# A decoder layer on one core: turning feed-forward tiles between output halves, and five smaller moves

## What is computed

```python
x = x + attention(layernorm(x), w_q_down, w_q_up_nope, w_q_up_rope, w_kv_down, w_k_rope, w_uk, w_uv, w_out)
x = x + cross_attention(layernorm(x), ctx_4096)
x = x + feed_forward(layernorm(x), k0, s0, k1, s1, k2, s2)

def feed_forward(x):                 # conn_dense(k, x) = x @ (+1 where k, -1 elsewhere)
    h = relu(s0 * conn_dense(k0, x)) * 2
    h = relu(ei_dense(h, k1, s1)) * 2     # the last fifth of the inputs is scaled by -4
    return ei_dense(h, k2, s2)
```

## Time and profile before

| what | value |
|---|---|
| median of three runs | 2095.1 us (2094.97 to 2096.36) |
| profiled execution: its time, its span | 2096.1 us, 2093.9 us |
| PE busy, PE weight loads busy | 2060.2 us, 1741.1 us |
| DVE, ACT, POOL busy | 1271.5, 775.7, 450.0 us |
| chain that ended last, by engine | PE 95%, DVE 2%, DMA 1%, ACT 1% |
| moved by DMA | 284.8 MB |

### The profile page before, as it was taken

The page is one execution under the profiler, slowest core; times in us unless marked ns, Lnnn a source line. Parts: engine busy times, 40 slices in busy tenths (PEclk is TensorE's granted clock), DMA queues, the critical chain, the costliest instruction groups (busy, mean ns, idle before and its releaser), DMA issues.

```text
span 2093.9 us, 30080 instructions
## 1 busy us (share of the span) xinstructions
PE 2060.2 (98%) x10746; PEld 1741.1 (83%) x10746; DVE 1271.5 (61%) x2114; ACT 775.7 (37%) x2018; POOL 450.0 (21%) x406
## 2 busy tenths in 40 slices
PE   6999999999999999999999999999999999999999
PEld 5787888888888888888888888888888868888887
DVE  4636666666666666666666666666667772333321
ACT  3324444444434353433333333333333455232221
POOL 2013333333324142321111211112121211000000
PEclk9999999999999999999999999999999999999999
DMA  5516343535353452666524234342444381202010
GB/s 211 239 66 224 105 174 105 195 115 205 123 183 121 157 178 100 224 223 215 170 90 150 85 120 135 118 142 70 150 132 184 124 310 49 81 1 81 1 41 40
DMA packets 63018, 284.78 MB, mean 136 GB/s; under 512 B 6641, under 2 KB 7281, under 8 KB 51441
## 3 DMA queue, kind: packets, MB, share of 16 engines
q1 hardware_dynamic: 62960, 284.00, 39.4%
HBM read 172.83 MB, written 111.15 MB: 136 GB/s over the span
## 4 chain that ended last, share of the span: by engine, by line
PE 95%; DVE 2%; DMA 1%; ACT 1%; issue 0%; POOL 0%; DVEq 0%; SPq 0%; POOLq 0%; ACTq 0%
PE at_out L53 11%; PE at_out L54 11%; PE at_out L55 11%; PE at_qbank L53 7%; PE at_qbank L55 7%; PE at_qbank L54 7%; PE at_qbank L967 6%; PE at_qbank L968 6%; PE at_score L756 4%; PE at_score L754 3%; PE at_turned L763 3%; PE at_value L55 2%; PE at_value L54 2%; PE at_value L53 2%; PE at_score L755 1%; PE at_turned L981 1%
## 5 line engine op out<-in xcount | busy, mean ns | idle before, releaser
L1564 DVE TENSOR_TENSOR at_acc<-at_out,at_acc 128x512 f32<-128x512 f32 x512 | 352.1, 688 | 116.0 <-PE at_out L55 109.3
L53 PE MATMUL at_out<-at_wvo,at_val_hi 128*128 128x512 f32 x1024 | 402.7, 393 | 1.7 <-DVE at_acc L1564 1.7
L54 PE MATMUL at_out<-at_wvo,at_val_hi 128*128 128x512 f32 x1024 | 400.9, 391 | 0.0
L55 PE MATMUL at_out<-at_wvo,at_val_lo 128*128 128x512 f32 x1024 | 399.8, 390 | 0.0
L1087 ACT ACTIVATE at_probs<-at_probs,at_row_stats 128x128 f32<-128x128 f32 x512 | 199.8, 391 | 358.4 <-DVE at_row_stats L1542 358.4
L1323 POOL TENSOR_TENSOR at_probs<-at_probs,at_row_stats 128x512 f32<-128x512 f32 x128 | 133.1, 1040 | 592.0 <-DVE at_row_stats L1547 592.0
L55 PEld LDWEIGHTS at_out<-at_wvo,at_val_lo 128*128 128x128 f32 x1024 | 192.3, 188 | 42.9
L53 PEld LDWEIGHTS at_out<-at_wvo,at_val_hi 128*128 128x128 f32 x1024 | 193.0, 188 | 37.0 <-DVE at_acc L1564 3.3
L54 PEld LDWEIGHTS at_out<-at_wvo,at_val_hi 128*128 128x128 f32 x1024 | 192.8, 188 | 32.4
L1093 ACT ACTIVATE at_pT_hi<-at_turned 128x512 fp32r<-128x512 f32 x128 | 76.4, 597 | 318.6 <-PE at_turned L763 318.6
L756 PE MATMUL at_score<-at_tok,at_qrope 128*128 128x256 f32 x512 | 170.5, 333 | 0.0
(11 more groups left out here) (193 smaller groups left out, 4344.1 us busy)
## 6 DMA issues: line engine op xcount, KB each, us to landing
wvo_d<-at_wvo SPq DMA_DIRECT2D x16, 2048.0 KB, 7.3
parts_d<-at_rope_parts SPq DMA_DIRECT2D x32, 1024.0 KB, 7.0
at_qrope<-parts_d SPq DMA_DIRECT2D x128, 256.0 KB, 5.0
at_wvo<-wvo_d SPq DMA_DIRECT2D x16, 2048.0 KB, 8.4
ab_raw<-in_w_heads SPq DMA_DIRECT2D x32, 576.0 KB, 4.7
cr_ctx<-in_context SPq DMA_DIRECT2D x16, 1024.0 KB, 7.7
wabs_d<-at_wabs SPq DMA_DIRECT2D x16, 768.0 KB, 7.6
at_wabs<-wabs_d SPq DMA_DIRECT2D x16, 768.0 KB, 5.3
```

The lines of the kernel that those rows point to most:

```text
L53: pe.matmul(out, w_hi, x_hi, start=first, stop=False)
L54: pe.matmul(out, w_hi, x_lo, start=False, stop=False)
L55: return pe.matmul(out, w_lo, x_hi, start=False, stop=last)
L1564: dve.tensor_tensor(at, outb[n][:], at, ALU.add).then_inc(added, 1)
```

## The change

Six edits, none of which alters the arithmetic.

1. Feed forward: the transposes of the next chunk's tile `t`, which stood after both output halves of tile `t`, now stand between half 0 and half 1. ACT's copies follow by their waits. DVE's two subtractions and the next tile's normalisation move ahead of the sum of half 1.
2. ACT, slot 0 of the full quads: `take_head` now comes ahead of the split of the rope weights.
3. The last chunk's tiles are stored in two halves of 512 columns, each as soon as it is summed.
4. SP loads all four x tiles ahead of the projection's first piece.
5. ACT takes the root of tile `t + 1` right behind the normalisation of tile `t`, and the first piece of the projection is split after the normalisation of tile 1 and the root of tile 2.
6. DVE: the moments of a first tile are cut into two halves, and the shift of the tile before stands between them.

```diff
             def preparation():                      # SP
-                load_x_tile(0, 0)
-                load_x_tile(0, 1)
+                for t in range(BPC):
+                    load_x_tile(0, t)
                 load_w_down(0)
-                load_x_tile(0, 2)
-                load_x_tile(0, 3)
                 sp.dma_start(ident[:], consts["ident"]).then_inc(ident_in, 16)
...
             for t in range(BPC):                    # SP, last chunk
-                sp.wait_ge(ff_summed, 2 * (BPC * c + t + 1))
-                sp.dma_start(out_chunks[c][:, t, :], ff_x[c % 2][:, t, :]).then_inc(y_out[c], 16)
+                for n in range(2):
+                    cols = slice(n * CH, (n + 1) * CH)
+                    sp.wait_ge(ff_summed, 2 * (BPC * c + t) + n + 1)
+                    sp.dma_start(out_chunks[c][:, t, cols], ff_x[c % 2][:, t, cols]).then_inc(y_out[c], 16)
...
             def feed_output(c, t):                  # PE
                 for n in range(2):
+                    if n and c + 1 < CHUNKS:
+                        for half in range(2):
+                            feed_turn(c + 1, t, half)
                     if t:
                         pe.wait_ge(ff_summed, 2 * BPC * c + 2 * (t - 1) + n + 1)
...
                     for t in range(BPC):
                         feed_output(c, t)
-                        if c + 1 < CHUNKS:
-                            for half in range(2):
-                                feed_turn(c + 1, t, half)
...
             def preparation():                      # ACT
+                root(0, 0)
                 for t in range(BPC):
-                    root(0, t)
                     first_normalise(t)
-                    if t == 0:
+                    if t + 1 < BPC:
+                        root(0, t + 1)
+                    if t == 1:
                         cut_w_down(0)
                 cut_w_down(1)
...
                         take_head(h, use[s] + 1, count)    # ACT, slot
+                if s == 0 and kind == "full":       # these stood ahead of take_pair and take_head
+                    act.wait_ge(wqr_raw_in, 16 * (m + 2))
+                    act.wait_ge(wqr_out, 16 * (m + 2))
+                    act.activation(wqr[:, 0], wqr_raw, ACT.Copy).then_inc(wqr_hi, 1)
...
             def preparation():                      # DVE
                 moments(0, 0)
-                first_shift(0)
-                moments(0, 1)
-                moments(0, 2)
-                first_shift(1)
-                moments(0, 3)
-                first_shift(2)
-                first_shift(3)
+                for t in range(1, BPC):
+                    half_moments(0, t, 0)
+                    first_shift(t - 1)
+                    half_moments(0, t, 1)
+                    whole_moments(0, t)
+                first_shift(BPC - 1)
...
                             dve.scalar_tensor_tensor(...).then_inc(ff_summed, 1)    # DVE, feed
-                        if c + 1 < CHUNKS:
-                            for half in range(2):
-                                feed_turn(c + 1, t, half)
-                            if t + 1 < BPC:
-                                feed_normalise(c + 1, t + 1)
+                            if n == 0 and c + 1 < CHUNKS:
+                                for half in range(2):
+                                    feed_turn(c + 1, t, half)
+                                if t + 1 < BPC:
+                                    feed_normalise(c + 1, t + 1)
```

More of the change, by code:

```diff
@@ L641, in _ @@
             for t in range(BPC):
-                sp.wait_ge(ff_summed, 2 * (BPC * c + t + 1))
-                sp.dma_start(out_chunks[c][:, t, :], ff_x[c % 2][:, t, :]).then_inc(y_out[c], 16)
+                for n in range(2):
+                    cols = slice(n * CH, (n + 1) * CH)
+                    sp.wait_ge(ff_summed, 2 * (BPC * c + t) + n + 1)
+                    sp.dma_start(out_chunks[c][:, t, cols], ff_x[c % 2][:, t, cols]).then_inc(y_out[c], 16)
             sp.wait_ge(y_out[CHUNKS - 2], 16)
-            sp.wait_ge(y_out[CHUNKS - 1], 16 * BPC)
+            sp.wait_ge(y_out[CHUNKS - 1], 16 * 2 * BPC)
         @block.tensor
@@ L1178, in slot @@
                     rope(m + 1, c, 16 * (m + 1 + c))
[L1179 to L1182, removed]
                 if part:
@@ L1435, in _, with half_moments, whole_moments, moments @@
         def _(dve):
[L1436 to L1439, removed]
+            def half_moments(i, t, h):
+                if h == 0:
+                    dve.wait_ge(x_in[i % 2][t], 16 * (i // 2 + 1))
+                dve.bn_stats(stats[:, t % 2, h, :], xt[i % 2][:, t, h * 512:(h + 1) * 512])
+            def whole_moments(i, t):
                 dve.drain()
                 dve.bn_aggr(mv[:, t, :], stats[:, t % 2].rearrange("p h s -> p (h s)")).then_inc(var_ready, 1)
+            def moments(i, t):
+                for h in range(2):
+                    half_moments(i, t, h)
+                whole_moments(i, t)
             def inverse(i, t):
```

## The result

The changed kernel takes 2087.92 us (median of 7 runs, 2086.4 to 2089.93) against 2094.97 us (2094.75 to 2096.36, also 7) on the same chip: ratio 0.9966, 95% interval 0.9955 to 0.9978, or 7.05 us less. The profiled execution took 2087.33 us with a span of 2085.1; against the one of before (2096.1 and 2093.9) that is 8.8 us less.

The account below looks back on a forecast made before the run. TensorE, busy 2060.2 of 2093.9 us, was taken as the bound, leaving 34 us idle to win. Terms 5.4 + 0.6 + 1.0 + 1.15 = 8.2 us took the median from 2095.1 to 2086.9, range 2085.0 to 2089.9.

Parts of the forecast that it names:

- The boundaries: Feed forward, three chunk boundaries: turning between output halves hides a 1.81 us TensorE stall at each, 5.4 us in all.
- the margin of tile 0: Feed forward: tile 0's normalised input is ready 0.6 us before its earlier transposes need it, the edit's smallest margin.
- The tail: End of kernel: storing the last tile in halves leaves 256 KB less to land after the last sum, saving 0.63 us.
- The start: First tiles: the fourth normalisation starts 1.36 us sooner; worth 0.7 to 1.36 us depending on TensorE's clock, taken as 1.0.
- Heads ahead of the split: Slot 1 of quad 0: evicting heads first moves the stall to values and output product, and wins 1.15 us.
- TensorE's release moves from 201.91 to 200.76: 1.15 us: Slot 1 of quad 0: the sums TensorE waits for come 1.15 us sooner, so TensorE goes on that much sooner.
- my second rival: Quad 0: the earlier head-weight store delays the raw rope weights; term -1.3 instead of 1.15, total 2089.4 us; chance 0.10.
- a stall of about 3 us was to remain: Slot 1 of quad 0, sign of being right: about 3 us of stall stays, ahead of values and sums.
- The later full quads: Six other full quads: the split delays ACT's high part by 0.84 us, covered by 2.0 us, so no loss.
- The stall goes whole: Rival, slot 1 of quad 0: the whole stall vanishes if raw weights land some 3 us earlier; 2084.0 us; chance 0.04.
- stall of twelve turns: Rival, feed forward: the normalised tile comes late for all 12 turns, 21.7 us lost, 2114.0 us; chance 0.02.
- wait of L929: Feed forward, sign of being wrong: a wait for the normalised tile; no size given.

Follow-up runs that it names:

- the experiment on the order: Kernel before with the new start order on ACT and VectorE, but x tiles 2 and 3 still loaded behind the projection's first piece: 2094.58 us, ratio 0.9997.
- The heads alone: Kernel before with only the head evictions moved ahead of the rope weights' split on ACT: 2094.41 us, ratio 0.9991.
- turns on TensorE only: Kernel before with TensorE's transposes between the output halves, VectorE keeping its old order with both sums first: 2099.96 us, ratio 1.0023.
- The two kernels with the weights early: Changed kernel with quad 1's raw rope weights issued earlier on SP: 2083.86 us; the same with the split ahead of the heads again: 2083.81 us.

## Why the prediction was right, point by point

The forecast was 2086.9 us, within 2085.0 to 2089.9, and the median is 2087.92.

- **The boundaries (5.4 us).** Right in place and size: 1.89 each in the profiled pair against 1.81, and 1.84 to 1.91 over all profiles. The stall went under half 1 with nothing late next, and the margin of tile 0 was 0.6 us as worked out. The experiment with VectorE's old order shows what the edit rests on: it is VectorE's turn behind the sum of half 0 that makes it work, and TensorE's new order without it loses.
- **The tail (0.63 us).** Right: 0.63 in the profiled pair, and the landing 2.0 us. The Trainium skill, DMA: Bandwidth & Descriptors, section Anatomy of one DMA, gives its numbers for the GpSimd path. With its fixed 2.0 us inside the 2.6 measured, a half would have taken 2.3 us, and the trace shows 2.0, so that fixed part doesn't hold for this queue. The prediction left out the same rule's second part, a time per byte, by which 256 KB less save 0.60 us as an estimate. The trace's 0.63 agrees with that. The size itself is read from traces alone, since the timed comparison is too coarse for it.
- **The start (1.36 us at the transposes, taken as 1.0).** The transposes came 1.56 us sooner, a little more than worked out: the first normalisation started at 7.15 instead of 7.25, and the step with the split took 1.96 instead of 2.05. There was no wait for data, and the experiment on the order shows that this was owed to the loads: without them 1.08 of the 1.56 us are lost to tile 2. What it is worth hung on the clock in the prediction, and the profiles bear that out for the old start only. In the first pair of profiles the rise came 8.64 and 8.57 us behind the transposes, in the second 5.97 and 6.06, so it moved with the start in both; but a third profile of before shows 8.11, so such a delay changes by itself by more than the start moved. In the first pair slot 1 of quad 0 began 1.76 us sooner, which is the whole 1.56 and 0.2 more. Over all profiles, seven with the old start began it at 187.92 to 188.99 (mean 188.44) and six with the new one at 187.04 to 187.39 (mean 187.24), 1.2 us sooner. From the first transposes to that slot the old start took 172.4 and 172.5 us where the rise came 6.5 and 6.0 us behind the transposes, and 172.8 to 173.2 where it came 8.0 to 8.6 behind. With the new start there is no such order: 173.05 with the rise at 8.57 and 173.07 to 173.6 with it at 5.6 to 6.8. The step on the clock is the one that failed here: with the new start an early rise only brings TensorE to a wait for a low part (1.14 us at 24.11 in the second profile of after). The 1.0 taken, the middle of two values for the clock, is near the 1.2 by luck.
- **Heads ahead of the split (1.15 us).** The mechanism was right, the size wrong. ACT stood at the same wait (4.23 us in place of 7.67), the high part started 0.75 us behind the split's start as worked out, and the stall moved to values and output. The sums came sooner by about the predicted amount: counted from the start of the slot, the first output product that waits for them was released at 200.00 - 188.99 = 11.01 us before, and at 197.00 - 187.23 = 9.77 after (9.86 in the second profile), 1.24 and 1.15 sooner.

  The step that failed is the next one, "TensorE's release moves from 201.91 to 200.76: 1.15 us". Between the two releases lie six matmuls, and before they took some 1.5 of the 1.91 us between the releases. After they ran at the low level and took 199.73 - 197.00 = 2.73. So TensorE came to the second place at 12.50 us into the slot, when the sums were there at about 11.7 (VectorE's sum of 198.17 ends at 198.86), and 0.8 of the 1.24 us were given back. In the second profile the fall came later: TensorE was at the second place at 12.11, but stayed at the low level behind it, and from there to the end of the slot it took 6.28 us instead of 5.58.

  Slot 1 took 18.17 and 18.39 us against 18.50, 0.33 and 0.11 less. In the old order the same fall costs nothing that shows, since TensorE waits for sums behind it: in the nine profiles with the old order slot 1 took 18.51 to 18.61 us in the four with a low clock there, and 18.50 to 18.67 in the five without. The heads alone, with the clock at 1.00, gave 17.73, still 0.4 more than the 17.35 worked out. There ACT had the raw weights 7.26 us behind their issue in place of 6.87 before (6.84 to 6.99 in the nine profiles with the old order), and that is the 0.4. Whether the earlier store did this (my second rival, at 0.4 in place of 2.45 us) is open: it was seen once, and in neither profile of the kernel after (6.79 and 6.86), where the store went out as early.

  Three readings of the prediction were off here, and the 1.15 rests on none of them. TensorE's waits in slot 1 add up to 2.43 + 0.79 + 0.25 = 3.5 us and not 4.1, since two of the four waits for sums are elsewhere; the slot as a whole took 4.3 more than the 14.2 it needs. SP's next issue behind the raw weights is the load of a second pair of heads (189.36), and only then the store. And a stall of about 3 us was to remain, where the slot still took 4.0 too long, 2.0 of them idle.
- **The later full quads (no loss).** Right: none of them waits for sums.
- **The stall goes whole** was rightly refused for this change: nothing issued the weights sooner. Issuing them sooner does it: 18.17 to 14.19 us.
- **No stall of twelve turns, no wait of L929**: neither is in the list.
- **The sum.** 8.2 predicted, 8.8 in the profiled pair (1.76 + 0.33 + 0.40 + 5.68 + 0.63), 7.05 by the medians. That the pair comes so near is in part luck: the start gave 0.76 more than was taken, 0.4 lies where no term was, the boundaries gave 0.25 more, and slot 1 gave 0.8 less. The later profile of after is 7.55 and 8.05 us faster than the two later ones of before. With slot 1 at 0.2 in place of 1.15 the sum is 7.3, near the medians, but this is an account and not shown: single executions of one kernel differ by more than the 1.75 us between pair and medians.

## What to carry to other kernels

When a wait is taken out by reordering the engine that waits, look at what else is queued behind the same late transfer, and then at why the transfer is late: here a new order on ACT gave under 1 us of a 4 us stall, and moving one DMA issue gave all of it. Turning the next input between two halves of an output hides its split under 3.6 us of matmuls, but only if the engine that splits is reordered with TensorE. And where TensorE binds behind a stall, the matmuls after it may run at half rate, so a stall of 2.0 us can cost 3.6.

## What the runs showed of the hardware that was not expected

- **The clock falls behind short stalls.** Behind 1.66 us of idle (slot 1) the granted clock went to the 1.2 GHz level in both profiles of the kernel after and not with the heads alone. Behind 2.04 us (turns on TensorE only) it did so at two boundaries of three, and in slot 1 of the old order, behind 2.4 to 2.6 us for the heads, in four profiles of nine. Behind the 1.57 us at the boundaries of before it did not at any of the 21 in seven profiles. So the length of the stall alone doesn't tell, and what decides isn't shown. The price is 0.20 us for each matmul of 512 columns at that level, 1.6 us for the eight at a boundary, and nothing where TensorE has to wait anyway.
- **A kernel with such stalls may spread; the runs don't settle it.** Of all runs of the kernel before, those with a mean granted clock of 1.000 have a median of 2095.41 us (11 runs), those at 0.999 2095.94 (42), those at 0.998 2097.82 (11). But these runs come from several chips, and ten of the last eleven from one of them. On another the order is the other way: 2095.34 at 1.000 (6 runs) and 2094.97 at 0.999 (16). The two kernels with the weights early showed 1.000 in every run, and lie within 1.2 and 1.3 us.
- **The rise at the start** (the first matmul of 512 columns that takes about 0.40 us in place of 0.63) came 5.6 to 8.6 us behind the first transposes in the fourteen profiles, at 19.5 to 24.4 us. With the old start an earlier rise is worth up to 0.8 us at slot 1 of quad 0 (172.4 to 173.2 us behind the transposes), with the new one nothing that shows: of the two profiles of after, the one with the fast level 2.5 us earlier had lost all of it 10 us later. The Trainium skill, TensorE: Matmul & The Clock Gate, section on the clock gate and the "warmup" mystery, says that the slow phase varies between runs of one kernel, since the chip's watch runs freely. The three profiles of before agree (8.64, 5.97 and 8.11 us).
